# Query projection of a first attention: the last 64 columns in three full-width matrix passes instead of five half-width ones, in a two-layer tower on one Trainium2 core

## The reference, cut to what matters

```python
h = tok_w[ids] + pos_w + type_w[mask]; h = layernorm(h) * gamma + beta
x = layernorm(h)                       # (8, 512, 192) in the source: 32 sequences of 128 here
q, k, v = x @ Wq, x @ Wk, x @ Wv       # 192 x 192 each
scores = q @ k.T, causal mask, softmax
h = h + attn @ v
...
logits = layernorm(h) @ phi_n.T        # 1024 slots, softmax over tokens and over slots
slots = dispatch.T @ layernorm(h)      # then 64 experts, the second attention, 8 routed experts
```

## Time and profile before

| | |
|---|---|
| time, median of 3 runs | 1421.07 us (1420.69 to 1423.09) |
| span of the profiled execution, first to last instruction | 1417.0 us |
| its mean granted TensorE clock | 0.988 of full speed |
| TensorE busy | 1344.6 us, 95% |
| VectorE busy | 972.1 us, 69% |
| ScalarE busy | 935.6 us, 66% |
| GpSimd busy | 253.8 us, 18% |

### The profile page before, as it was taken

The page is one execution under the profiler, slowest core; times in us unless marked ns, Lnnn a source line. Parts: engine busy times, 40 slices in busy tenths (PEclk is TensorE's granted clock), DMA queues, the critical chain, the costliest instruction groups (busy, mean ns, idle before and its releaser), DMA issues. The chain is left out here.

```text
span 1417.0 us, 29741 instructions
## 1 busy us (share of the span) xinstructions
PE 1344.6 (95%) x9102; PEld 1192.6 (84%) x9102; DVE 972.1 (69%) x2952; ACT 935.6 (66%) x2208; POOL 253.8 (18%) x284
## 2 busy tenths in 40 slices
PE   8899999998999999999999999799999999879995
PEld 6688888886899989989999998688888888768895
DVE  6977777555777777777777774488888888622321
ACT  1477778787566666666666665388888888735551
POOL 5422100000111111111111110102122122121344
PEclk9999999999999999999999999999999999989998
DMA  6144443455666666666666665545454457016641
GB/s 201 41 148 155 150 150 139 150 187 191 189 196 197 184 196 194 188 188 191 198 184 193 199 181 167 163 144 160 144 155 148 151 153 212 12 43 152 155 74 18
DMA packets 181636, 221.05 MB, mean 156 GB/s; under 512 B 25348, under 2 KB 148458, under 8 KB 181536
## 3 DMA queue, kind: packets, MB, share of 16 engines
q1 hardware_dynamic: 147904, 179.52, 41.1%
q10 hardware_dynamic: 25952, 33.32, 7.1%
q0 software_dynamic: 7680, 6.95, 2.6%
HBM read 142.36 MB, written 79.90 MB: 157 GB/s over the span
## 5 line engine op out<-in xcount | busy, mean ns | idle before, releaser
L1239 PE MATMUL bank<-e_w,e_h_full 128*128 128x192 f32 x1920 | 324.7, 326 | 0.4
L1239 PEld LDWEIGHTS bank<-e_w,e_h_full 128*128 128x128 f32 x1920 | 310.6, 190 | 1.7 <-ACT e_h_full L1312 1.3
L1312 ACT ACTIVATE e_h_full<-bank,e_b 128x512 f32<-128x512 f32 x240 | 165.0, 688 | 189.6 <-PE bank L60 189.6
L1173 POOL TENSOR_TENSOR e_ln_rstd<-e_ln_var_eps,minus_half 128x4 f32<-128x4 f32 x62 | 62.5, 1008 | 449.5 <-DVE e_ln_var_eps L1362 449.5
L1720 ACT ACTIVATE probs<-bank,head_neg_max 128x128 f32<-128x128 f32 x384 | 134.9, 392 | 7.7 <-DVE head_neg_max L1816 5.7
L1369 DVE TENSOR_SCALAR e_rows<-e_slot_sums,e_ln_mean_var,e_ln_rstd 128x192 f32<-128x192 f32 x248 | 77.5, 376 | 77.6 <-POOL e_ln_rstd L1173 77.6
L1282 ACT ACTIVATE e_x_full<-bank,e_ln_shift,e_ln_gain 128x512 f32<-128x512 f32 x124 | 89.7, 773 | 46.1 <-PE bank L1211 44.2
L995 PE MATMUL bank<-x,dispatch_weights 128*128 128x193 f32 x512 | 95.5, 329 | 6.4 <-ACT slot_stage L842 5.7
L703 DVE TENSOR_REDUCE column_neg_max<-bank 128x4 f32<-128x512 f32 x64 | 44.2, 691 | 78.1 <-PE bank L60 78.0
L60 PE MATMUL bank<-e_x_hi,e_w1hi 128*128 128x512 f32 x216 | 95.0, 440 | 2.8 <-ACT e_h_full L1312 1.7
L1600 PE MATMUL bank<-slot_outputs_then_w_part,combineT 128*128 128x193 f32 x512 | 92.5, 333 | 2.7 <-ACT combineT L1712 2.1
(11 more groups left out here) (274 smaller groups left out, 3089.3 us busy)
## 6 DMA issues: line engine op xcount, KB each, us to landing
slot_sums<-slot_stage SPq DMA_DIRECT2D x64, 386.0 KB, 3.2
e_slot_sums<-slot_sums SPq DMA_DIRECT2D x64, 386.0 KB, 3.6
slot_outputs<-e_stage ACTq DMA_DIRECT2D x64, 384.0 KB, 3.1
slot_outputs_then_w_part<-slot_outputs SPq DMA_DIRECT2D x32, 768.0 KB, 5.0
e_w<-in_w SPq DMA_DIRECT2D x64, 288.0 KB, 3.0
slot_logits<-kept_logits SPq DMA_DIRECT2D x32, 512.0 KB, 3.0
slot_logits<-slot_logits SPq DMA_DIRECT2D x32, 512.0 KB, 3.4
e_w1raw<-in_w SPq DMA_DIRECT2D x80, 192.0 KB, 2.7
```

The lines of the kernel that those rows point to most:

```text
L1173: pool.tensor_tensor(rs[u][:], ve[u][:], half[:], ALU.pow).then_inc(rstd_ready, 1)
L1239: last = pe.matmul(ybank(u)[:, j // 2, (j % 2) * D:(j % 2 + 1) * D], hf[:, k, js], w2s[u][:, k, :], start=k == 0, stop=k == MT - 1)
L1312: act.activation(hf[:, m, :], hbank(u, m), act_fn, bias=b1s[:, m, ds(n, 1)]).then_inc(acted, 1)
```

## The change

M is kept in two pieces. Its first 128 columns are split as before into `M_hi` and `M_lo`, now 128 columns wide. The rounded part and the rest of its last 64 columns stand side by side in one operand of 128 columns, `M_rest_hi_and_lo`. The passes of `queries(a, 1)` therefore give 128 rows: rows 0 to 63 the product with the rounded weights, rows 64 to 127 that with the rest. Both are taken by the same three passes, and their sum is left to the scores, whose contraction now runs over 128 rows with `xT`'s repeated features. (The product of the two rests, left out before, is now in it.)

```diff
-        Mhi, Mlo = sb("M_hi", [P, 2, D], F32R), sb("M_lo", [P, 2, D], F32R)
+        Mhi, Mlo = sb("M_hi", [P, 2, P], F32R), sb("M_lo", [P, 2, P], F32R)
+        M_rest = sb("M_rest_hi_and_lo", [P, 2, 2 * DR], F32R)
...
-        qT0, qT1 = sb("qT0", [P, GB * P]), sb("qT1", [DR, GB * P])
+        qT0, qT1 = sb("qT0", [P, GB * P]), sb("qT1_two_parts", [P, GB * P])
...
                             dve.wait_ge(M_hi_ready, 1)
-                            dve.tensor_tensor(Mlo[:], T["M"][:], Mhi[:].bitcast(F32), ALU.subtract
-                                              ).then_inc(M_split, 1)
+                            dve.tensor_tensor(Mlo[:], T["M"][:, :, 0:P], Mhi[:].bitcast(F32), ALU.subtract)
+                            dve.tensor_tensor(M_rest[:, :, DR:], T["M"][:, :, P:D], M_rest[:, :, 0:DR].bitcast(F32),
+                                              ALU.subtract).then_inc(M_split, 1)
...
-                act.activation(Mhi[:], T["M"][:], ACT.Copy).then_inc(M_hi_ready, 1)
+                act.activation(Mhi[:], T["M"][:, :, 0:P], ACT.Copy)
+                act.activation(M_rest[:, :, 0:DR], T["M"][:, :, P:D], ACT.Copy).then_inc(M_hi_ready, 1)
...
-                        take(q_done, 2 * a + 2, qT1[:], b4[0:DR], q_took)
+                        take(q_done, 2 * a + 2, qT1[:], b4, q_took)
...
-                    c, b = ((slice(0, P), b7), (slice(P, D), b4))[k]
-                    matmuls(pe, b[0:c.stop - c.start], [
-                        (Mhi[:, 0, c], xThi[:, 0, :]), (Mlo[:, 0, c], xThi[:, 0, :]), (Mhi[:, 0, c], xTlo[:]),
-                        (Mhi[:, 1, c], xTboth[:]), (Mlo[:, 1, c], xTboth[:])]).then_inc(q_done, 1)
+                    if k == 0:
+                        last = matmuls(pe, b7, [
+                            (Mhi[:, 0, :], xThi[:, 0, :]), (Mlo[:, 0, :], xThi[:, 0, :]), (Mhi[:, 0, :], xTlo[:]),
+                            (Mhi[:, 1, :], xTboth[:]), (Mlo[:, 1, :], xTboth[:])])
+                    else:
+                        last = matmuls(pe, b4, [
+                            (M_rest[:, 0, :], xThi[:, 0, :]), (M_rest[:, 0, :], xTlo[:]), (M_rest[:, 1, :], xTboth[:])])
+                    last.then_inc(q_done, 1)
...
-                        last = matmuls(pe, b7[:, c], [(qT0[:, c], xT[:, 0, c]), (qT1[:, c], xT[0:DR, 1, c])])
+                        last = matmuls(pe, b7[:, c], [(qT0[:, c], xT[:, 0, c]), (qT1[:, c], xT[:, 1, c])])
```

## The result

The changed kernel takes 1409.76 us (median of 4 runs, 1409.19 to 1411.17) against 1421.92 (median of 4) for the kernel before on the same chip (1420.69 to 1423.09): the ratio is 0.9914, 95% interval 0.9898 to 0.993. Timed once more on another occasion it was 0.9909 (0.9892 to 0.9926). The forecast was 1419.6 and its range ended at 1417.3, so the change brought some 12 us where 1.4 were expected.

What follows compares the result with a forecast made beforehand. TensorE is busy 95%, but a ScalarE and VectorE chain was taken to bound the stretch around the queries. Terms 0.47 + 0 + 0 + 0 + 0.60 + 0.44 − 0.07 = 1.44 us less: 1421.07 to 1419.6, range 1417.3 to 1421.9.

Steps and rivals of the forecast that it cites:

- taller operands: Scores and query copies with 128 instead of 64 rows: both costed at nothing, from their bands of durations.
- Two passes fewer: Queries of each group: three full-width passes, 0.70 us, replace five taking 1.14, freeing 0.44 us of TensorE at full clock.
- What is kept of it in groups 2 to 7: Share of the freed TensorE time kept: groups 2 and 3 nothing, 4 to 6 0.20 us each, 7 all 0.44.
- The chain of ScalarE and VectorE: Before slot 2's slot sums in group 5: 12.2 us of ScalarE and VectorE work that waits for no queries.
- The waits of group 2: TensorE's wait for ScalarE's staging at slot 2's slot sums, claimed to grow from 0.48 to 0.92 us.
- Group 0: First group, TensorE at 1.2 GHz: scores start earlier, gain 0.47 us, bounds 0 to 0.86.
- Group 1: Second group: scores wait for ScalarE's query copy, behind a rounding waiting for VectorE, so 0 kept.
- the recorded sign of being wrong: TensorE's clock (PEclk) falling below 1.00 between 66 and 343 us would show the prediction wrong.
- The split of M: Start-up on VectorE: a second instruction pays the fixed part again, loss 0.07 us, upper bound 0.14.
- From the span to the time: Whole kernel: 4.07 us around the profiled span, taking 1415.6 to a time of 1419.6.
- TensorE-bound after all: Rival for the tower: all the passes' saving is kept, 3.87 us, time 1417.2; chance 0.10.
- the third rival: Growing TensorE waits lower its clock, 1.4 us a stretch; chance 0.08 for one or two, 0.03 for more.

Runs made afterwards that it cites:

- tall scores with five passes: The kernel before with scores contracting over 128 rows (upper rows of qT1 zero), queries keeping five 64-row passes: 1411.59 us, ratio 0.9932.
- short scores with three passes: The changed kernel with three full-width query passes kept, but scores over only rows 0 to 63 of qT1: 1421.27 us, ratio 0.9997.
- the spare passes: The changed kernel with two filler passes of 128x512 ahead of the three query passes in each group: 1411.26 us, ratio 0.9921.

## Why the prediction was wrong, step by step

**The step that failed** is *taller operands*: "I cost both at nothing", with the reason that scores of 64 and of 128 rows lie in one band of durations. The band was right and was the wrong thing to read, since a duration holds the time for the result to get through; and only its median was looked at, while 57 of the 128 durations lie at 373 to 377 ns, all but one of them a record right behind a turn, and in tall scores with five passes only one does. The text itself says that a pass costs the distance between starts. Had I applied it, the row of group 0 gives 3.30 for 16 records, 0.2 each, while four turned weights of the same type and size lie ahead of a neighbour without a wait at 0.43, 0.11 each. Sixteen at 0.11 are 1.7; the excess of 1.5 us a group stood in the trace. Measured, the taller operands were worth 1.52 us in each of groups 2 to 7, 9.6 there in all, with five passes kept. It is also the step with a rule against it in the Trainium skill that I had not looked up (TensorEngine Tiling (Array Packing), Key Properties): "Mode switching requires drain". If a change of row height counts as such a switch, the traces agree that it has a price, 0.19 us at matmuls of 128 columns and 0.16 at 512; that the price is a drain they don't show. For a change of width they show no price: before the change, in group 6, the first 64-column pass starts 0.24 behind its full-width neighbour and the first full-width pass 0.23 behind the last narrow one, the pace without a turn.

```profile
229.94 0.40 PE L60 MATMUL bank<-e_x_hi_over_lo,M_lo 128*128 128x512 f32 x1
230.18 0.39 PE L60 MATMUL bank<-e_x_hi,M_hi 128*64 128x512 f32 x1
...
231.09 0.39 PE L60 MATMUL bank<-e_x_hi_over_lo,M_lo 128*64 128x512 f32 x1
231.32 0.40 PE L60 MATMUL bank<-x_hi,phi_hi 128*128 128x512 f32 x1
```

**Two passes fewer**, 0.44 us of TensorE: right, 1.14 became 0.70. **What is kept of it in groups 2 to 7**, 0 + 0 + 0.6 + 0.44 = 1.04: right in size. The passes were worth 1.7 there with short scores, 1.1 on top of tall ones, and 0.9 over the whole tower as seen with the spare passes. The shares were less right: with short scores groups 2 to 7 kept 0.0, 0.4, 0.1, 0.1, 0.1 and 1.0, where 0, 0, 0.2, 0.2, 0.2 and 0.44 were put; why group 7 kept more than its passes save is open. The chain of ScalarE and VectorE that this rests on was right: in short scores with three passes and in the changed kernel the slot sums wait about 0.27 for the staging in group 5. The waits of group 2 were put at 0.92; in the profile after the slot sums wait 0.62 and the turned weights ahead of them 0.26, together 0.88. The same chain fits with the scores' saving being kept whole and that of the passes not: the passes stand ahead of TensorE's wait for the staging, the scores behind it.

**Group 0**, 0.47: its distance to group 1 fell by 1.12, to 20.72, in both traces of the changed kernel. VectorE's whole wait of 1.02 went; in the first trace the clock was up as well, in the second it was down and the shorter scores did it. What the passes alone give under the low clock, the case that the 0.47 was worked out for, no run shows. **Group 1**, 0: it kept nothing and lost some. ScalarE's copy sets the start of its scores as predicted, but the distance from its queries to those of group 2 grew from 32.51 to 32.67, and to 33.38 in the second trace. This goes with a stretch of lower clock that the trace before doesn't have; the next such stretch stands at the start of the expert phase. Clock of TensorE in the profile after:

```profile
core 0: us, PE busy (x), PEclk, DMA share, GB/s
64.00:67.00 3.00, 3.00 (x11) 0.50 0.00 0
340.00:343.00 3.00, 2.81 (x7) 0.54 0.64 134
```

So the recorded sign of being wrong, a clock below 1.00 between 66 and 343 us, came true at both ends of that range, with little weight in the result.

**The split of M**, 0.07: right, by the spacing and not by the 0.16 of the Trainium skill's formula (VectorE: DVE Perf Modes, section on the TRN2 errata).

**From the span to the time**, 4.07: not what lies around the execution. That is about 1.7: the second trace of the kernel before has a span of 1417.4 in a run of 1419.06. By this the profiled execution took about 1418.7, below the three timed ones, and the other 2.4 are spread. It did no harm, since the gain was taken off the median.

**The rivals.** TensorE-bound after all came nearest in time, by luck: its reason, that the passes' 3.87 would all be kept, was wrong, as short scores with three passes show. The clock did what the third rival feared, mostly elsewhere. (The Trainium skill's remark on transposes that this rival cites stands in Part 4 of the page, not in Part 1.) The same sixteen matmuls early in the combine phase, in the trace before, then after, then after once more:

```profile
900.42 2.86 PE L1600 MATMUL bank<-slot_outputs_then_w_part,combineT 128*128 128x193 f32 x16 [1.47 <-ACT combineT L1712]
```

```profile
890.01 4.41 PE L1607 MATMUL bank<-slot_outputs_then_w_part,combineT 128*128 128x193 f32 x16 [1.46 <-ACT combineT L1719]
```

```profile
890.46 4.54 PE L1607 MATMUL bank<-slot_outputs_then_w_part,combineT 128*128 128x193 f32 x16 [1.47 <-ACT combineT L1719]
```

They are 1.55 and 1.68 longer, at the lower clock, behind the same wait as before; the mean clock from 880 to 1000 us is 1.00, 0.99 and 0.97 in the three traces. All seven traces whose tower is at least 5.8 us shorter show this stretch; the three others don't. Whether the earlier start brings it on was not tried.

From the first matmul of the expert phase to the end, the spans of before take 1065.2 and 1065.8, those of the changed kernel 1068.0 and 1069.4, and those of the other experiments 1066.8 to 1070.9. So in the profiled executions 3 to 4 us of the tower's 11.6 and 10.9 were given back behind it, 1.55 and 1.68 of that in the sixteen matmuls shown. The medians of the timed runs fell by 12.2 and 13.4, so they don't show this loss. The likely reason is that both profiled executions of the kernel before lie at the low end of its spread: its 37 timed runs beside the experiments go from 1417.9 to 1425.5 us, those up to 1418.9 at a mean granted clock of 0.988 to 0.990 and those from 1423.5 on at 0.983 to 0.985. Where in the latter the clock was low is not known; no profile was taken of such a one.

## What to carry to other kernels

Price a matmul by the distance between starts, never by its duration, and compare that distance with the best of the same shape anywhere in the trace; here 0.20 against 0.11 a record stood there before the change. Keep neighbouring matmuls at one contraction height: fill the short operand with zeros, or with something useful as here, or order them so that the heights turn seldom. Two freed passes in a stretch that another engine's chain bounds are worth only the slack of that chain, and an experiment with each half of a change alone tells which half paid.

## What the runs showed of the hardware that I had not expected

- A turn of the contraction height between neighbouring matmuls costs 0.19 us for float32 records of 128 columns and 0.16 us for passes of 512, in both cases half ahead of the first pass of the new height and half behind it. In the trace it shows as a weight load that starts with its own matmul, not 0.11 ahead of it.
- A turn of the output height (64 or 128 weight columns) costs nothing that the spacing shows: 0.23 to 0.24.
- A matmul over 64 rows of contraction is as fast as one over 128 among its like: 1.98 us for sixteen with two turns, 1.71 for sixteen tall ones.
- Whether the cost is a full drain of the array or only the load that isn't taken ahead can't be told from these records, and was not tried.
